# Two-layer graph network with routed feed-forward: the first weight product taken from the rows of x to the products with adj

## The reference

```python
def gnn(x, adj, W1, b1, W3, b3, Wf, bf):          # W1, W3, Wf: 256 x 256
    h = relu(adj @ (x @ W1) + b1)
    h = relu(adj @ (h @ W3) + b3)
    return tanh(h @ Wf + bf)

x = x + gnn(layernorm(x), adj, ...)
y = layernorm(x)
w, idx = top_k(y @ gate_w, 2); w = softmax(w)      # 8 experts
x = x + sum over the two experts e of w_e * ((silu(y @ EW1[e]) * (y @ EW3[e])) @ EW2[e])
```

## Time and profile before

| | us |
|---|---|
| median of 3 timed runs (lowest, highest) | 733.09 (731.18, 733.44) |
| span of the profiled execution | 728.6 |
| own time of the profiled execution | not listed beside its span |
| TensorE busy, products | 638.1 (88%) |
| TensorE busy, weight loads | 539.6 (74%) |
| VectorE busy | 382.1 (52%) |
| ScalarE busy | 321.2 (44%) |
| GpSimd busy | 141.9 (19%) |
| chain that ended last: TensorE, VectorE, DMA | 72%, 11%, 5% |

### The profile page before, as it was taken

How to read it: one execution, slowest core, us unless ns; L and a number is a source line. 1 busy time by engine, 2 the same in 40 slices (tenths; PEclk the granted TensorE clock), 3 DMA queues, 4 the chain that set the end, 5 groups by cost and what they waited for, 6 DMA issues and landing times.

```text
span 728.6 us, 11905 instructions
## 1 busy us (share of the span) xinstructions
PE 638.1 (88%) x3501; PEld 539.6 (74%) x3502; DVE 382.1 (52%) x842; ACT 321.2 (44%) x649; POOL 141.9 (19%) x117
## 2 busy tenths in 40 slices
PE   1999999999995969746699879999998999999992
PEld 1988888888773756624478668888887888888882
DVE  3875444556467786878554133363666363333330
ACT  1567465774550645515253133264555353333330
POOL 3000000000015030360466731111111111111111
PEclk9999999999996989965599979999999999999996
DMA  8982000000060100606145321142565111011111
GB/s 296 349 337 116 1 0 1 30 1 0 1 241 19 59 29 31 230 6 226 51 134 186 94 30 16 14 127 71 184 187 186 15 14 14 9 13 14 14 14 16
DMA packets 32294, 61.54 MB, mean 84 GB/s; under 512 B 2978, under 2 KB 24868, under 8 KB 30212
## 3 DMA queue, kind: packets, MB, share of 16 engines
q1 hardware_dynamic: 25060, 51.13, 19.7%
q0 software_dynamic: 6912, 9.70, 7.7%
q10 hardware_dynamic: 288, 0.26, 0.1%
HBM read 52.05 MB, written 9.04 MB: 84 GB/s over the span
## 4 chain that ended last, share of the span: by engine, by line
PE 72%; DVE 11%; issue 7%; DMA 5%; POOL 2%; ACT 2%; SPq 0%; ACTq 0%; DVEq 0%; POOLq 0%
PE bank L1236 34%; PE bank L1121 7%; PE bank L1123 7%; PE bank L1122 7%; PE bank L1097 4%; PE bank L1281 3%; PE bank L1160 3%; DVE m_run L859 3%; DMA xg<-ffn_in_rows,idx 3%; DMA adj_s<-in_adj 2%; DVE ring L732 2%; POOL xg L443 2%; PE bank L1134 2%; PE bank L1085 2%; PE bank L1176 1%
## 5 line engine op out<-in xcount | busy, mean ns | idle before, releaser
L1236 PE MATMUL bank<-ew,xeT 128*128 128x512 f32 x840 | 204.1, 400 | 3.1 <-DVE ew L1011 1.1
L1236 PEld LDWEIGHTS bank<-ew,xeT 128*128 128x128 f32 x840 | 158.2, 192 | 35.8 <-issue 3.9
L732 DVE TENSOR_TENSOR ring<-adj_s,ring 128x512 fp32r<-128x512 f32 x128 | 93.5, 735 | 79.2 <-ACT adj_s L507 41.2
L1121 PE MATMUL bank<-ring,Z 128*128 128x512 f32 x256 | 112.1, 438 | 17.6 <-DVE ring L732 17.3
L1236 PE MATMUL bank<-ew,heT 128*128 128x256 f32 x840 | 112.6, 292 | 6.3 <-issue 4.1
L1236 PEld LDWEIGHTS bank<-ew,heT 128*128 128x128 f32 x840 | 106.0, 197 | 8.2 <-issue 8.1
L1123 PE MATMUL bank<-ring,Z 128*128 128x512 f32 x256 | 103.1, 403 | 0.0
L459 POOL DMA_INDIRECT out<-y_st,idx_st x35 | 54.4, 1556 | 250.0 <-issue 237.8
L1122 PE MATMUL bank<-ring,Z 128*128 128x512 f32 x256 | 102.5, 400 | 0.0
L1031 DVE TENSOR_TENSOR heT<-bank,heT 128x512 fp32r<-128x512 f32 x70 | 45.2, 686 | 94.6 <-ACT heT L643 94.4
L636 ACT ACTIVATE sil<-bank 128x512 f32<-128x512 f32 x70 | 41.7, 597 | 111.5 <-PE bank L1236 111.0
(11 more groups left out here) (161 smaller groups left out, 729.3 us busy)
## 6 DMA issues: line engine op xcount, KB each, us to landing
w_raw<-in_L_ffn_W SPq DMA_DIRECT2D x24, 1024.0 KB, 5.5
adj_s<-in_adj SPq DMA_DIRECT2D x16, 1024.0 KB, 6.3
x_in<-in_x SPq DMA_DIRECT2D x4, 512.0 KB, 4.7
x_res<-in_x SPq DMA_DIRECT2D x4, 512.0 KB, 3.5
out<-x SPq DMA_DIRECT2D x4, 512.0 KB, 2.9
ffn_in_rows<-x_res SPq DMA_DIRECT2D x4, 512.0 KB, 3.1
xg<-ffn_in_rows,idx POOLq DMA_INDIRECT x39, 2.8
out<-y_st,idx_st POOLq DMA_INDIRECT x35, 3.8
```

Source lines behind the costliest of these rows:

```text
L732: nc.vector.tensor_tensor(lo, src, hi, ALU.subtract).then_inc(s_lo, 1)
L1121: nc.tensor.matmul(a, zh, hi, start=(jb == 0), stop=False)
L1236: last = nc.tensor.matmul(out_ap, stat[:, sl, k, :], w_at(k, wl), start=(k == k0 and sl == wl == 0), stop=(k == k1 - 1 and sl == 1))
```

## The change

The first layer is computed as (adj @ norm(x)) @ W1. Z of the first layer is norm(x) itself, split into high and low in groups of four tiles: ScalarE rounds 128 x 1024 at once (`x_hi`), VectorE subtracts as a fourth part of `x_norm`. `x_T`, `z1_rows` and their splits are gone. Each chunk's accumulated block is rounded into aT at steps 0 and 1 of the next chunk (`a_hi`), its low part taken at steps 1 and 2 (`a_lo`), and multiplied by W1 behind the product of step 3 (`h_rows`: twelve products of 512 columns, into the two banks `sm`). `hidden1` reads those banks at steps 4 and 5, `h_lo` comes at step 6, `z2_rows` at 7 and 8. aT and hTs share the same bytes. The last four tiles of z2 are split from PSUM into Z without a copy between, at steps 8 and 9. SP's wait before the last two adj tiles is now on the split of x.

```diff
@@ scalar
-            def z1_hi(t):
-                act.wait_ge(s_zp, t + 1)
-                nc.scalar.copy(Z[:, 0, t, :], sm[t % 2][:, 0:D]).then_inc(s_zhi, 1)
+            def x_hi(g):
+                act.wait_ge(s_xn, g + 1)
+                nc.scalar.copy(Z[:, 0, CT * g:CT * (g + 1), :], x_in[:, CT * g:CT * (g + 1), :]).then_inc(s_zhi, CT)
...
-            def hidden1(c, f):
+            def a_hi(c, f):
                 act.wait_ge(s_mm, NT * (c + 1))
...
+                nc.scalar.copy(aT[:, 0, f, :], acc[c % 2][f][:, :]).then_inc(s_a, 1)
+
+            def hidden1(c, f):
+                act.wait_ge(s_hp, KD * (c + 1))
                 for out_f in (hTs[:, 0, f, :], hTf[:, 1, f, :]):
-                    last = nc.scalar.activation(out_f, acc[c % 2][f][:, :], ACT.Relu, bias=bT[:, 0, f:f + 1])
+                    last = nc.scalar.activation(out_f, sm[f][:, :], ACT.Relu, bias=bT[:, 0, f:f + 1])
...
-                if s < NT - 1:
-                    if s < NT - 2:
-                        x_T(s + 2)
-                    z1_hi(s + 1)
-                if NT <= s < S1 + NT and jb in (1, 2):
-                    hidden1(s // NT - 1, jb - 1)
+                if NT <= s < S1 + NT and jb in (0, 1):
+                    a_hi(s // NT - 1, jb)
+                if NT <= s < S1 + NT and jb in (4, 5):
+                    hidden1(s // NT - 1, jb - 4)
@@ vector
+                if part == 3:
+                    dve.wait_ge(s_zhi, CT * (g + 1))
+                    tiles = slice(CT * g, CT * (g + 1))
+                    nc.vector.tensor_tensor(Z[:, 1, tiles, :], x_in[:, tiles, :], Z[:, 0, tiles, :].bitcast(F32),
+                                            ALU.subtract).then_inc(s_zlo, CT)
...
-                if s < NT - CT - 1 and (s + 1) % CT < 3:
+                if s < NT - CT - 1:
                     x_norm(1 + (s + 1) // CT, (s + 1) % CT)
...
-                    if jb == 3:
+                    if jb in (1, 2):
+                        a_lo(before, jb - 1)
+                    if jb == 6:
                         h_lo(before)
-                    if jb in (5, 6):
-                        z2_out(CT * before + 2 * jb - 10)
-                        z2_out(CT * before + 2 * jb - 9)
+                    if jb in (8, 9):
+                        for t in (CT * before + 2 * jb - 16, CT * before + 2 * jb - 15):
+                            if t < NT - CT:
+                                z2_out(t)
+                            else:
+                                z_lo(t)
@@ tensor
+            def h_rows(c):
+                pe.wait_ge(s_w1s, 1)
+                pe.wait_ge(s_alo, KD * (c + 1))
+                if c >= 1:
+                    pe.wait_ge(s_z2, CT * c)
+                for f in range(KD):
+                    for k in range(KD):
+                        for al, wl in ((0, 0), (0, 1), (1, 0)):
+                            last = nc.tensor.matmul(sm[f][:, :], W1s[:, wl, k, f * P:(f + 1) * P], aT[:, al, k, :],
+                                                    start=(k == al == wl == 0), stop=(k == KD - 1 and al == 1))
+                    last.then_inc(s_hp, 1)
...
-                if s < NT - 1:
-                    if s < NT - 2:
-                        x_T(s + 2)
-                    z1_rows(s + 1)
                 if s + 2 < S1:
                     transpose_block(s + 2)
                 product(s)
-                if NT <= s < S1 + NT and jb in (4, 5):
-                    z2_rows(CT * (s // NT - 1) + 2 * jb - 8)
-                    z2_rows(CT * (s // NT - 1) + 2 * jb - 7)
+                if NT <= s < S1 + NT and jb == 3:
+                    h_rows(s // NT - 1)
+                if NT <= s < S1 + NT and jb in (7, 8):
+                    z2_rows(CT * (s // NT - 1) + 2 * jb - 14)
+                    z2_rows(CT * (s // NT - 1) + 2 * jb - 13)
```

More of the change, by code:

```diff
@@ L59, in gnn_and_routed_ffn @@
         Z = at("Z", [P, 2, NT, D], F32R, 128)
-        z2 = at("z2", [P, NT, D], F32, 160)
-        W1s = at("W1s", [P, 2, KD, D], F32R, 160)
-        xTs = at("xTs", [P, 2, 2, KD, P], F32R, 168)
+        z2 = at("z2", [P, NT - CT, D], F32, 160)
+        W1s = at("W1s", [P, 2, KD, D], F32R, 172)
+        aT = at("aT", [P, 2, KD, CW], F32R, 176)
         x_res = at("x_res", [P, CT, D], F32, 160)
@@ L207, in gnn_and_routed_ffn @@
         s_xt = sem("s_xT")
-        s_xtlo = sem("s_xT_lo")
+        s_xall = sem("s_x_normal")
+        s_a = sem("s_aT_hi")
+        s_alo = sem("s_aT_lo")
+        s_hp = sem("s_h_psum")
         s_w1s = sem("s_W1_split")
-        s_zp = sem("s_z_psum")
         s_zhi = sem("s_z_hi")
@@ L341, in _ @@
                 if t == NT - 2:
-                    sp.wait_ge(s_zp, NT)
+                    sp.wait_ge(s_zlo, NT)
                 sp.dma_start(adj_s[:, t, :], adj_rows[t, :, :]).then_inc(s_adj[t % 2], 16)
@@ L358, in _ @@
                     sp.wait_ge(s_xn1st, 16 * (c + 1))
-                    sp.wait_ge(s_xtp, NT + CT * (c + 1))
+                    sp.wait_ge(s_xtp, CT * (c + 1))
                     residual(c + 1)
@@ L535, in z_hi @@
             def z_hi(t):
+                if t >= NT - CT:
+                    act.wait_ge(s_z2p, t + 1)
+                    act.wait_ge(s_mm, S1)
+                    nc.scalar.copy(Z[:, 0, t, :], sm[t % 2][:, 0:D]).then_inc(s_zhi, 1)
+                    return
                 act.wait_ge(s_z2, t + 1)
@@ L552, in token_work @@
                     for i in (2 * k - 20, 2 * k - 19):
-                        act.wait_ge(s_xtp, NT + CT * c + i + 1)
+                        act.wait_ge(s_xtp, CT * c + i + 1)
                         nc.scalar.copy(xT[:, i, :, :],
@@ L569, in _ @@
             roots(1)
-            x_T(0)
-            x_T(1)
-            z1_hi(0)
+            x_hi(0)
             for s in range(2 * S1):
@@ L579, in _ @@
                     roots(2 + s // CT)
+                if s < NT - CT and s % CT == 2:
+                    x_hi(1 + s // CT)
                 if s == CT:
@@ L593, in _ @@
                     z_hi(jb - 2)
-                if layer == 1 and c == 0 and 7 <= jb < 7 + CT:
-                    z_hi(NT - CT + jb - 7)
+                if layer == 1 and c == 0 and jb in (8, 9):
+                    z_hi(NT - CT + 2 * jb - 16)
+                    z_hi(NT - CT + 2 * jb - 15)
                 if layer == 1 and c >= 2:
@@ L735, in z_lo, with a_lo @@
                 dve.wait_ge(s_zhi, NT + t + 1)
-                nc.vector.tensor_tensor(Z[:, 1, t, :], z2[:, t, :], Z[:, 0, t, :].bitcast(F32),
+                src = sm[t % 2][:, 0:D] if t >= NT - CT else z2[:, t, :]
+                nc.vector.tensor_tensor(Z[:, 1, t, :], src, Z[:, 0, t, :].bitcast(F32),
                                         ALU.subtract).then_inc(s_zlo, 1)
+            def a_lo(c, f):
+                dve.wait_ge(s_a, KD * c + f + 1)
+                nc.vector.tensor_tensor(aT[:, 1, f, :], acc[c % 2][f][:, :], aT[:, 0, f, :].bitcast(F32),
+                                        ALU.subtract).then_inc(s_alo, 1)
             def h_lo(c):
@@ L904, in _ @@
             dve.wait_ge(s_const, 3)
-            for part in range(3):
+            for part in range(4):
                 x_norm(0, part)
@@ L1065, in _ @@
             pe.wait_ge(s_w1, 16)
[L1067 to L1084, removed]
-                        last = nc.tensor.matmul(sm[t % 2][:, 0:D], xTs[:, t % 2, xl, k, :], W1s[:, wl, k, :],
-                                                start=(k == xl == wl == 0), stop=(k == KD - 1 and xl == 1))
-                last.then_inc(s_zp, 1)
             def transpose_block(s):
@@ L1104, in product @@
                 pe.wait_ge(s_lo, s + 1)
-                if n == 0:
-                    pe.wait_ge(s_zlo, jb + 1)
+                if n == 0 and jb % CT == 0:
+                    pe.wait_ge(s_zlo, jb + CT)
                 if n == NC:
@@ L1110, in product @@
                     if n - 2 < NC:
-                        pe.wait_ge(s_h1, KD * (n - 1))
+                        pe.wait_ge(s_alo, KD * (n - 1))
                     else:
@@ L1129, in z2_rows @@
                 pe.wait_ge(s_hlo, c + 1)
-                if t >= 2:
+                if t >= NT - CT + 2:
+                    pe.wait_ge(s_zlo, NT + t - 1)
+                elif t >= 2:
                     pe.wait_ge(s_z2, t - 1)
@@ L1155, in token_work @@
                         if c == 0:
-                            pe.wait_ge(s_z2, NT)
+                            pe.wait_ge(s_zlo, 2 * NT)
                             pe.wait_ge(s_bf, 1)
@@ L1171, in token_work @@
                     for i in (2 * k - 22, 2 * k - 21):
-                        pe.wait_ge(s_xt, NT + CT * c + i + 1)
+                        pe.wait_ge(s_xt, CT * c + i + 1)
                         if c >= 1:
@@ L1186, in token_work @@
                         slot_map(c, n)
-            for t in range(2):
-                x_T(t)
-            z1_rows(0)
             transpose_block(0)
```

26 lines of the change are left out of this document (1 added, 25 removed).

## The result

| | kernel before | changed kernel |
|---|---|---|
| median of the timed runs, first comparison | 733.27 (731.18 to 740.62, 4 runs) | 742.76 (740.05 to 745.58, 4 runs) |
| ratio, 95% interval | | 1.0153 (1.0077 to 1.023) |
| measured again, median | 731.56 (23 runs) | 739.05 (6 runs) |
| ratio, 95% interval | | 1.0095 (1.0062 to 1.0129) |
| span of the profiled execution | 728.6 | 738.7, its own time 740.51 |

What follows compares the result with a forecast made beforehand. TensorE's issued work was taken to bound the stretch from 18 to 188 us. First chunk -11.6, then +4.5, +4.5, +5.4 and +5.3 for chunks 0 to 3, make +8.1 on 733.1: 741.2 us, range 737.0 to 745.5.

Steps and rivals of the forecast that it cites:

- TensorE's sum: TensorE's issued work: first chunk gains 11.6 us net; twelve W1 products add 2.8 us per chunk, 11.1 in all.
- VectorE's share of the first chunk: First chunk: statistics, normalization, subtraction and blocks take VectorE 8.1 us against TensorE's 7.33 per four steps, giving back 2.6.
- The sign I had named: First chunk: blocks' transposes 1.9 to 2.0 us apart up to step 11, with idle time ended by VectorE.
- The wait for aT: Start of next chunk: accumulator rounding ahead of block 1 delays TensorE 0.35 us, or 0.7 in the second half.
- The wait for the ReLUs: Behind each chunk's W1 products: ReLUs ahead of block 5 cost 1.0 us, the second pair 0.3; second half 1.4.
- this hand-off: Chunk 3's, in the second half: waits for aT, ReLUs, h's subtraction and last Z tiles, carried on as 3.4 us.
- The 4.5 us "over the span": Whole kernel before: median of three timed runs, 733.1 us, lies 4.5 over the profiled execution's span of 728.6.
- A busy share misread: From 18 to 188 us: TensorE almost always busy at granted clock 1.00, VectorE and ScalarE at 55 to 77%.
- That hand-offs cost nothing: Rival, at the chunk hand-offs: the ring of three blocks carries TensorE through the ReLUs; 729.2 to 731.8 us; chance 4%.
- cheap wide products: Rival, at the W1 products: a 512-wide product costs about 131 ns, giving 736.4 us; chance 2%.
- Half the waits: Rival: first chunk at full pace and half of the 9 us of waits, time within 2 us of now; chance 5%.
- That the clock falls in the new gaps: Rival, at five places where TensorE stands still: lower clock adds at most 6 us, 742 to 747; chance 9%.

Runs made afterwards that it cites:

- The fuller order: The two moves plus, in the first chunk, x's rounding and subtraction one block later and next statistics filling the wait; 0.9963 of the kernel before.
- the second profile: The changed kernel measured again without any edit; time 1.0095 of the kernel before, median 739.05 us.
- the move alone: Changed kernel with only the roundings into aT (and their subtractions) one step later; first product with Wf 2.1 us earlier, time 1.0075 of the kernel before.
- the two moves: Changed kernel with ReLUs (and what follows them) and roundings into aT each one step later; 0.9982, repeated 0.9985, of the kernel before.
- the doubling: Changed kernel with the twelve W1 products of each chunk issued twice, ReLUs waiting for the second round; time 1.0238 of the kernel before.

## Why the prediction was right

**TensorE's sum.** The first chunk gained 11.0 in the first profile, where the clock stayed low for longer, and 11.7 in the second; 11.6 was forecast. The W1 products cost 2.73 for a group in the chain (2.8 forecast) and 10.8 when added once more (11.1 forecast).

**VectorE's share of the first chunk** (2.6 forecast). The size held, the working was only half right. I had it as a busy sum of 8.1 against 7.33 for four steps. The fuller order leaves that sum as it is and takes 1.6 us of the time away, so most of it was the round trip, which my sum held only as 0.35 to 0.4 for a group. That the size came out is in part luck. The sign I had named, transposes 1.9 to 2.0 apart up to step 11, did not appear: they are 1.83 apart with single gaps. In the first profile it was the slow products of the start that were paid, not VectorE: behind them the transposes of steps 5 to 13 come 1.83 apart, and only those of step 14 come 0.55 late, behind block 11. I had named the slow start as hidden by VectorE; in that execution it was rather the other way round. The group 1 of x also landed later there: its statistics start 2.0 us behind the first transposes, where I took the 1.35 of before and the second profile has 1.3.

**The wait for aT** (0.35 and 0.7 forecast). ScalarE waits for the last product of the chunk ahead of block 17:

```profile
53.41 0.59 ACT L513 CAST aT<-bank 128x512 fp32r<-128x512 f32 x1 [2.09 <-PE bank L1101]
```

The transposes of steps 19 and 20 are 2.21 apart in place of 1.83: 0.38. In all 2.1 by the move alone, 1.75 by my terms.

**The wait for the ReLUs** (1.35 a chunk forecast). The transposes of steps 22 to 25 are 2.48, 2.23 and 2.13 apart in place of 1.83, together 1.35. In the second half 1.4 were forecast for the first block:

```profile
172.03 0.69 ACT L519 ACTIVATE hTs<-bank,bT 128x512 fp32r<-128x512 f32 x1 [4.84 <-PE bank L1113]
...
172.62 0.68 ACT L519 ACTIVATE hTf<-bank,bT 128x512 f32<-128x512 f32 x1
...
173.19 0.61 ACT L503 CAST ring<-adj_s 128x512 fp32r<-128x512 f32 x1
...
173.84 0.69 DVE L729 TENSOR_TENSOR ring<-adj_s,ring 128x512 fp32r<-128x512 f32 x1 [5.92 <-ACT ring L503]
...
174.59 0.50 PE L1099 MATMUL bank<-ring,Z 128*128 128x512 f32 x1 [1.23 <-DVE ring L729]
```

Products of 512 columns for the second half of block 68 and the first of block 69 start at 172.51 and 174.59, where 0.68 apart is the pace: 1.40 lost, 1.23 of it as idle time that VectorE's block ended, and ahead of that ScalarE's two ReLUs and its rounding. My terms for this hand-off add up to 3.3 and not to the 3.4 that I carried on, so the sum should have been 8.0; the measured stretch is 5.6 where I had 5.3.

**Prices bounded from rows that were near.** The 1024-wide rounding was an estimate of 1.04, the subtraction 1.22, the rounding of the accumulator as any other (columns as in the earlier trace rows):

```profile
L717 DVE TENSOR_TENSOR Z<-x_in,Z 128x1024 fp32r<-128x1024 f32 x4 | 4.9, 1226 | 3.6 <-ACT Z L488 3.6
...
L513 ACT CAST aT<-bank 128x512 fp32r<-128x512 f32 x8 | 4.8, 598 | 8.3 <-PE bank L1101 8.3
L488 ACT CAST Z<-x_in 128x1024 fp32r<-128x1024 f32 x4 | 4.2, 1047 | 4.3 <-DVE x_in L711 4.3
```

1.047, 1.226 and 0.598 us.

**The total.** 733.1 + 8.1 puts the difference on the median of the timed runs, so the span doesn't enter it. The 4.5 us "over the span" were misread, though: the profiled execution of the changed kernel took 740.51 for its span of 738.7, only 1.8 more. By that the profiled execution of the kernel before took about 730.4 (an estimate, 728.6 + 1.8), and the other 2.7 is how far it was below the median. The forecast of 741.2 lies between the two medians of the changed kernel.

**A busy share misread.** ScalarE and VectorE do not stand at 55 to 77% in all three stretches: VectorE has 46.66 of 97 us in the middle one, 48%. No term rests on it. The granted clock of 1.00 was misread too. Up to 22.18 us the trace of the kernel before has no clock entry, and its first transposes were slow; the sum held, because it took its prices for steps and products from later ones.

**The rivals.** That hand-offs cost nothing is ruled out by the chain and by the two moves; cheap wide products by the doubling. Half the waits is ruled out by the table of stretches, whose terms are within 0.3 of the forecast behind the first chunk. That the clock falls in the new gaps is not borne out: the products at 56.25 and later, right behind a gap, keep their 0.23, and the clock record has one single entry, full clock, from 26.21 to 231.01. Only the start was slow. The price that I gave this rival, 4 x 1.4, counts one slow block at each place where the text says two; by its own words it is 11 us, not 6.

## What to carry to other kernels

Where a producer engine works in program order, count what stands behind a waiting instruction, not only what the instruction costs. Here some 11 us of added products were paid for by 11.0 to 11.7 saved, and nearly the whole loss of 8 us came from two kinds of instruction that waited one place too early in ScalarE's order. Put a wait behind the work that is ready, one block later, and the same arithmetic costs nothing more. Before work goes to an idle engine, try whether the two disturb each other: look for an instruction that suddenly takes three times its length.

## What the runs showed of the hardware that I had not expected

- A VectorE subtraction with two SBUF operands took 2.05 us in place of 0.69 while GpSimd ran one of its own (2.37 us), and ended 0.54 behind it.
- The moment at which the clock rises differs between executions of one kernel. In one profile of the changed kernel it is 26.21 us, in the other 24.09; the second block of products starts 3.44 us behind the first in the one (21.53 to 24.97) and 3.11 in the other (21.33 to 24.44), and the first chunk ended 0.7 sooner in the second.
- A granted clock of 1.00 in a stretch can mean that the trace has no clock entry there. At the start the spacing of like instructions tells: transposes 0.21 apart before the first entry and 0.11 behind it.
- TensorE's work from 9.6 to 12.9 us in the kernel before did not spare its first eight transposes at 18 us the slow pace (1.94 us). Idle transposes did: from 9.4 to 17.2 us in the changed kernel (1.06), from 13.0 to 18.2 in the kernel before (1.04).
